# Recommender tower on one core: two more tables looked up by matmul at the start, gathered units prepared four blocks ahead, and the folded Gram values turned by DMA

## What is computed

```python
e = jnp.stack([tbl_f[ids[:, f]] for f in range(26)], axis=1)        # (2048, 26, 128)
all_emb = jnp.concatenate([r_bottom_output[:, None, :], e], axis=1)
gram = jnp.einsum('bfd,bgd->bfg', all_emb, all_emb)
z = gram[:, _TRIU_I, _TRIU_J]                                        # (2048, 351)
h = jnp.concatenate([z, r_bottom_output], axis=1)                    # (2048, 479)
h = jnp.maximum(h @ W_top1 + b_top1, 0.0)                            # 512
h = jnp.maximum(h @ W_top2 + b_top2, 0.0)                            # 256
y = h @ W_top3                                                       # 1
```

## Time and profile before

| | |
|---|---|
| median of 3 runs | 356.62 us (356.36 to 359.17) |
| the profiled execution | 355.85 us, of which the span is 354.1 us |
| busy: TensorE, VectorE, ScalarE, GpSimd | 329.4, 245.1, 205.0, 255.7 us |
| TensorE's granted clock | full throughout |
| DMA | 42.88 MB, 121 GB/s on average |

### The profile page before, as it was taken

One profiled execution on the slowest core, in us unless ns is written; L12 is line 12 of the kernel. 1 busy time (PEld: TensorE's weight loads), 2 busy tenths in 40 slices (PEclk: granted clock), 3 DMA queues, 4 the chain that ended last, 5 costly groups with the idle time before them and its releaser, 6 DMA issues.

```text
span 354.1 us, 13649 instructions
## 1 busy us (share of the span) xinstructions
PE 329.4 (93%) x5840; PEld 295.9 (84%) x5840; DVE 245.1 (69%) x720; ACT 205.0 (58%) x349; POOL 255.7 (72%) x274
## 2 busy tenths in 40 slices
PE   0788989999999999999999989999999999999996
PEld 0676979998888989979888889879999798888885
DVE  1999989996676978459763987549885597431412
ACT  3684777522345659549478567565865587572222
POOL 5777777777777777777777777777777777777720
PEclk9999999999999999999999999999999999999999
DMA  6668649422228685576685496584769476532210
GB/s 206 189 173 219 184 127 316 121 55 54 55 54 159 95 165 114 83 155 136 148 115 98 98 175 123 121 99 99 158 125 141 99 130 113 115 83 56 56 31 1
DMA packets 64203, 42.88 MB, mean 121 GB/s; under 512 B 48784, under 2 KB 56464, under 8 KB 64016
## 3 DMA queue, kind: packets, MB, share of 16 engines
q1 hardware_dynamic: 55024, 24.38, 34.8%
q0 software_dynamic: 8448, 17.32, 20.8%
q10 hardware_dynamic: 672, 0.33, 0.3%
HBM read 31.24 MB, written 0.01 MB: 88 GB/s over the span
## 4 chain that ended last, share of the span: by engine, by line
PE 82%; DVE 9%; DMA 3%; ACT 2%; issue 2%; SPq 0%; ACTq 0%; DVEq 0%
PE hot_ps L498 30%; PE gram_ps L476 14%; PE h_ps L530 11%; PE xt_ps L498 9%; PE h_ps L575 8%; DVE onehot L731 5%; PE h_ps L527 4%; PE xt_ps L459 3%; DMA rows_sb<-in_rows_dram 2%; DVE tab L798 2%; PE zt_ps L512 2%; DMA ids_wide<-in_hot_ids_dram 1%; DVE h L788 1%; ACT turned L993 1%; DVE Z L739 1%
## 5 line engine op out<-in xcount | busy, mean ns | idle before, releaser
L445 POOL DMA_INDIRECT X<-in_table_dram,rows_sb x264 | 254.3, 963 | 82.8 <-issue 78.9
L731 DVE TENSOR_SCALAR onehot<-ids_wide,row_value 128x288 fp32r<-128x288 int16 (+2 forms) x575 | 183.9, 390 | 31.6 <-PE hot_ps L498 20.6
L498 PE MATMUL hot_ps<-onehot,tab 128*128 128x288 f32 (+2 forms) x948 | 144.6, 305 | 14.1 <-DVE onehot L731 13.8
L498 PEld LDWEIGHTS hot_ps<-onehot,tab 128*128 128x128 f32 x948 | 132.0, 190 | 17.7 <-issue 15.4
L706 ACT COPY XT<-turned 128x512 int16<-128x512 int16 x82 | 65.7, 885 | 8.7 <-DMA turned<-planes 8.7
L883 ACT COPY XT<-hot_ps 128x288 f32<-128x288 f32 (+2 forms) x66 | 40.1, 658 | 39.8 <-PE hot_ps L498 37.5
L476 PEld LDWEIGHTS gram_ps<-XT 128*27 128x27 f32 x4096 | 45.1, 104 | 20.9 <-issue 15.8
L476 PE MATMUL gram_ps<-XT 128*27 128x26 f32 x4096 | 56.3, 192 | 4.2 <-issue 1.2
L872 ACT COPY planes<-X 128x1024 int16<-128x1024 int16 x41 | 44.3, 1082 | 17.5 <-DMA X<-in_table_dram,rows_sb 17.5
L530 PE MATMUL h_ps<-stage_sb,w_sb 128*128 128x256 f32 (+3 forms) x192 | 44.2, 366 | 0.0
L530 PEld LDWEIGHTS h_ps<-stage_sb,w_sb 128*128 128x128 f32 (+1 forms) x192 | 35.0, 191 | 4.3
(11 more groups left out here) (54 smaller groups left out, 137.8 us busy)
## 6 DMA issues: line engine op xcount, KB each, us to landing
stage_sb<-in_hot_dram SPq DMA_DIRECT2D x20, 256.0 KB, 3.5
X<-in_table_dram,rows_sb POOLq DMA_INDIRECT x264
ids_wide<-in_hot_ids_dram SPq DMA_DIRECT2D x8, 360.0 KB, 5.3
ids_wide<-in_hot_ids_dram SPq DMA_DIRECT2D x4, 400.0 KB, 4.0
bottomT<-in_bottom_t_dram SPq DMA_DIRECT2D x8, 128.0 KB, 3.9
w_sb<-in_w_dram SPq DMA_DIRECT2D x1, 1024.0 KB, 7.0
turned<-planes SPq DMA_TRANSPOSE x41
stage_sb<-in_hot_dram SPq DMA_DIRECT2D x5, 128.0 KB, 2.9
```

What stands on the lines that cost most here:

```text
L445: pool.indirect_dma_start(X[:, n % RING, k, :], None, table, bass.IndirectOffsetOnAxis(idx[:, column:column + 1], 0)).then_inc(gathered[n ...
L498: mm = pe.matmul(hot_bank(i)[:, 0:width(n)], tab[u][:, part, D * c:D * (c + 1)], onehot[p % ONEHOTS][:, c - BITES[u][h], 0:width(n)], star ...
L731: compared = dve.tensor_scalar(onehot[p % ONEHOTS][:, c - BITES[u][h], 0:width(n)], ids_wide[:, k, 0:width(n)], row_value[:, c:c + 1], Non ...
```

## The change

Sizes. GATHERED stays 16; EXTRA is 2, so 8 hot tables are looked up in the head (140 products) and 2 are gathered for its eight blocks, by one SIDE unit of four gathers into a view of Z, with its own indices (`side_sb`). 260 gathers in all. Order of the units: 0, 1, SIDE, 2, ... 63; turned in the head behind tables 1, 2, 4, 6 and 7. The hot tables' pieces start with two of 2 chunks for table 0; 6 instead of 12 pieces are split behind the head, in 3 steps.

Ahead. Units are split, turned and, where TensorE turns them, transposed in step b for block b+4 (LEAD) instead of b+2 and b+1. Blocks 10 to 59 go by DMA.

Folded values. For tiles 0 to 12 ScalarE splits the folded columns into 16-bit halves (`split_z`), SP starts a DMA transpose (`turn_z`, behind the unit's turn), and VectorE puts the halves together in ZT by two int16 copies. Tiles 13 to 15 go by TensorE as before.

TensorE. All blocks to 55 go in pairs (`pair`), strips always in runs of 16; both layer-1 products or both layer-2 products of a step stand on end. Layer 2 has half a bank for each tile of a pair, and VectorE works in that half instead of in SBUF. The last eight blocks are reordered. VectorE's memset of gram_ps and the addition to the long list of row numbers move behind other work in the head.

```diff
-ALWAYS = 16
-SOMETIMES = 4
-HOT = TABLES - ALWAYS
-HOT_BASE = HOT - SOMETIMES
+GATHERED = 16
+EXTRA = 2
+HOT = TABLES - GATHERED
+HOT_BASE = HOT - EXTRA
 FOUR = 4
 BLOCKS = P // PAD
-TILE_COLUMNS = BLOCKS * (1 + ALWAYS // FOUR)
-BOTTOM_SLOT = ALWAYS + SOMETIMES
+TILE_COLUMNS = BLOCKS * GATHERED // FOUR
...
-SPLIT_STEPS = 6
+SPLIT_STEPS = 3
...
+LEAD = 4
+SIDE = UNITS
+STREAM = [0, 1, SIDE] + list(range(2, UNITS))
+HEAD_TURNS = {1: 0, 2: 1, 4: SIDE, 6: 2, 7: 3}
+Z_BY_DMA = TILES - 3
+TURN_FROM, TURN_TO = 10, UNITS - BLOCKS
+BY_DMA = list(range(TURN_FROM, TURN_TO))
+DIRECT = [n for n in STREAM if n not in BY_DMA]
 NTH = {n: k for order in (DIRECT, BY_DMA) for k, n in enumerate(order)}
+MOVED = {n: k + 1 for k, n in enumerate(STREAM)}
...
+            def turn_z(t):
+
+                sp.wait_ge(z_split, t + 1)
+                wait(sp, zt_moved, t)
+                sp.dma_start_transpose(z_turned[:].rearrange("p h c s -> p (h c) s"),
+                                       z_planes[:].rearrange("p h c s -> p (h c s)")).then_inc(z_turned_in, 16)
...
+            for b in range(LAST):
                 n = GROUP_OF[b]
+                if b == STARTS[n + 1] - 3 and n + 2 < GROUPS:
+                    load_low_ids(n + 2)
+                if b == STARTS[n] and 0 < n < GROUPS - 1:
                     load_high_ids(n + 1)
+                if b + LEAD in BY_DMA:
+                    turn(b + LEAD)
+                if b % BLOCKS == 0 and 0 < b // BLOCKS <= Z_BY_DMA:
+                    turn_z(b // BLOCKS - 1)
...
+            for n in STREAM:
+                if n == BLOCKS:
                     pool.wait_ge(idx_ready, 1)
+                if n == SIDE:
+                    pool.wait_ge(side_ready, 1)
+                    for k in range(FOUR):
+                        pool.indirect_dma_start(side[:, k, :], None, table,
+                                                bass.IndirectOffsetOnAxis(side_sb[:, k:k + 1], 0)
+                                                ).then_inc(side_gathered, 16)
+                    continue
                 before = n - RING
                 if before >= 0 and before in BY_DMA:
                     pool.wait_ge(planes_ready, NTH[before] + 1)
                 elif before >= 0:
                     pool.wait_ge(xt_full, NTH[before] + 1)
                 for k in range(FOUR):
-                    column = TILE_COLUMNS * t + (k if j is None else BLOCKS + FOUR * j + k)
+                    column = FOUR * n + k
...
+                if begin == 0 and (t % 2 == 0 or t >= TILES - 2):
+                    wait(pe, prod_done, t)
...
+            def layers(t, j):
 
                 g = t // 2 - 1
+                if g < 0:
+                    return
+                if t % 2 == 0 and j == 2:
+                    layer1(g, 0)
+                    layer1(g, 1)
+                if t % 2 == 1 and j == 0:
+                    layer1(g, 2)
+                    layer1(g, 3)
+                if t % 2 == 1 and j == 2:
+                    layer2(2 * g)
+                    layer2(2 * g + 1)
+
+            def pair(b):
+
                 t, j = b // BLOCKS, b % BLOCKS
+                between = t >= 2 and (t % 2 == 1 or j == 2) and b + 2 < LAST
+                if between:
                     lookups(*slice_of(b))
+                    strips(b, 0, 1)
+                    layers(t, j)
+                    strips(b, 1, RUNS)
                 else:
                     for run in range(RUNS):
                         lookups(*slice_of(b, run, run + 1))
+                        strips(b, run, run + 1)
+                if b + LEAD < TURN_FROM:
+                    transposes(b + LEAD)
+                for run in range(RUNS):
+                    lookups(*slice_of(b + 1, run, run + 1))
+                    strips(b + 1, run, run + 1)
+                if not between:
+                    layers(t, j)
+                if j == 0 and t > 0:
+                    z_transposes(t - 1)
+                if b + 1 + LEAD < TURN_FROM:
+                    transposes(b + 1 + LEAD)
...
             def last_blocks():
+                b, t = LAST, TILES - 2
                 pe.wait_ge(hot_placed, 1 + max(i for i in range(len(LOOKUPS)) if hot_bank(i) is xt_ps))
+                strips(b)
+                strips(b + 1, 0, 1)
                 z_transposes(t - 1)
+                strips(b + 1, 1, RUNS)
                 layer1(len(JOBS) - 3, 0)
                 layer1(len(JOBS) - 3, 1)
+                strips(b + 2, 0, 1)
+                transposes(b + 4)
+                strips(b + 2, 1, RUNS)
                 layer1(len(JOBS) - 3, 2)
                 layer1(len(JOBS) - 3, 3)
+                strips(b + 3, 0, 1)
+                transposes(b + 5)
+                strips(b + 3, 1, RUNS)
                 layer2(t - 2)
+                z_transposes(t)
+                layer2(t - 1)
                 b, t = LAST + BLOCKS, TILES - 1
+                strips(b, 0, 1)
+                transposes(b + 2)
+                strips(b, 1, RUNS)
                 layer1(len(JOBS) - 2, 0)
                 layer1(len(JOBS) - 2, 1)
+                strips(b + 1)
                 layer1(len(JOBS) - 2, 2)
                 layer1(len(JOBS) - 2, 3)
+                transposes(b + 3)
+                strips(b + 2)
+                strips(b + 3)
                 bottoms_last(0, C1 - 1)
+                layer2(t - 1)
                 z_transpose_last(0)
                 z_transpose_last(1)
                 bottoms_last(C1 - 1, C1)
...
             def move_zt(t):
 
                 g, at = JOB_OF[t]
-                dve.wait_ge(zt_full, t + 1)
+                if t >= Z_BY_DMA:
+                    dve.wait_ge(zt_full, t + 1 - Z_BY_DMA)
+                else:
+                    dve.wait_ge(z_turned_in, 16 * (t + 1))
                 if t == 0:
                     dve.wait_ge(part1, FIRST_PIECE[HOT])
                 wait(dve, h1_full, C1 * (g - 1))
+                if t < Z_BY_DMA:
+                    for h in range(2):
+                        moved = dve.tensor_copy(ZT_words[g % 2][:, :, at, :, h], z_turned[:, h, :, :])
+                    moved.then_inc(zt_moved, 1)
+                    return
...
-                dve.wait_ge(h2_full, t + 1)
+                dve.wait_ge(h2_full, t + 1 if t >= TILES - 2 else t + 2 - t % 2)
                 wait(dve, prod_done, t)
-                dve.tensor_tensor(h2[:], h2_ps[:, 0:N2], vec_sb[:, 0, :], ALU.add).then_inc(h2_moved, 1)
+                h2 = h2_half(t)
+                dve.tensor_tensor(h2, h2, vec_sb[:, 0, :], ALU.add).then_inc(h2_moved, 1)
                 dve.wait_ge(h2_moved, t + 1)
-                dve.scalar_tensor_tensor(h2[:], h2[:], 0.0, vec_sb[:, 1, :], ALU.max, ALU.mult,
+                dve.scalar_tensor_tensor(h2, h2, 0.0, vec_sb[:, 1, :], ALU.max, ALU.mult,
...
             for q in range(FIRST_PIECE[HOT_BASE]):
-                split_second(q)
+                if q == FIRST_PIECE[1]:
+                    dve.wait_ge(side_loaded, 16)
+                    dve.tensor_tensor(side_sb[:, 0:FOUR], side_sb[:, 0:FOUR], side_sb[:, FOUR:2 * FOUR], ALU.add
+                                      ).then_inc(side_ready, 1)
+                    dve.wait_ge(rows_loaded, 16)
+                    dve.tensor_tensor(chunks[:, 1:, :], chunks[:, 1:, :],
+                                      starts.to_broadcast([P, TILES - 1, TILE_COLUMNS]), ALU.add).then_inc(idx_ready, 1)
                 for p in asked_of(q):
                     one_hot(p)
+                split_second(q)
+            dve.memset(gram_ps[:], 0.0).then_inc(pads_zero, 1)
...
+            def split_z(t):
+
+                if t == 0:
+                    act.wait_ge(z_pads_zero, 1)
+                act.wait_ge(folded_all, t + 1)
+                wait(act, z_turned_in, 16 * t)
+                pairs = folded[:].rearrange("p r c -> p (r c)")[:, HALF:HALF + PAIRS]
+                act.copy(z_planes[:].rearrange("p h c s -> p h (c s)")[:, :, 0:PAIRS],
+                         pairs.bitcast(i16).rearrange("p (e h) -> p h e", h=2)).then_inc(z_split, 1)
...
+                for i in placed_in(b):
+                    if i not in ended(b):
+                        place_hot(i)
                 for p in pieces_ended(b):
+                    if is_last(p) and ASKED[p][0] in placed_in(b):
+                        place_hot(ASKED[p][0])
                     one_hot_share(p + ONEHOTS)
+                if j == 0 and 0 < t <= Z_BY_DMA:
+                    split_z(t - 1)
+                split_words(b + LEAD)
                 if j == 2:
                     place_bottom(t + 1)
                 for q in LATE_PIECES[PER_STEP * b:PER_STEP * (b + 1)]:
                     split_first(q)
+                if b + LEAD < TURN_FROM:
+                    move(b + LEAD)
+                if b + LEAD - 1 in BY_DMA:
+                    move(b + LEAD - 1)
...
+                place_bottom(TILES - 1)
                 relu(len(JOBS) - 3, 0)
                 relu(len(JOBS) - 3, 1)
```

(11 more changed lines are left out.)

339 lines of the change are left out of this document (130 added, 209 removed).

## The result

The changed kernel took 370.88 us, the kernel before on the same chip 357.89: a ratio of 1.0378, 95% interval 1.0343 to 1.0412. It is slower by 3.8%. I had forecast 352.8 us and a range from 350.9 to 356.8. The profiled execution has a span of 369.8 us against 354.1, 15.7 us more. The profiled execution before took 355.85 us, less than its median, and the one of the changed kernel 371.86, more than its median; so the medians differ by 13.0 us only.

A forecast was written before the change was run, and what follows sets the result against it. Two chains, GpSimd's gathers and TensorE's own work, were taken to arrive together, the gathers deciding after the change. Last turn 337.2 + 12.8 + 0.3 gave a 350.3 us span against 354.1, in proportion 352.8 us; range 350.9 to 356.8.

The forecast's parts named there:

- Turns: TensorE, block 0 to the last turn: 9 of 22 unit turns remain, at 0.40 us each, -5.2 us.
- Transposes of folded: TensorE, block 0 to the last turn: 13 transposes of 0.31 us a tile go, -4.0 us.
- The 0.52 us waits at layer 2: TensorE: layer 2's second tile no longer waits for h2_moved, with half a bank for each tile, -2.1 us.
- The tail: Behind the last turn: 12.8 us remain as before, plus 0.3 us for the last tile's transposes.
- The gather stream: GpSimd: four gathers fewer -5.0, waits for TensorE -1.0, slower gathers +1.5; sum -4.5 us, last gather over at 334.9 us.
- part 4: End of the kernel: last unit's landing and the path from block 60's unit, 15.4 us, put the last turn at 337.2 us.
- The head: TensorE up to block 0: two more tables looked up, sum +7.8 us, block 0 at 39.3 instead of 31.5 us.
- The chain in order takes over: Rival in SP's queue: z_turned waits behind turn(b+4), delaying VectorE's one-hots; 2 to 4 us of gain lost; chance 0.12.
- TensorE's 5 us as spare: End of the kernel: TensorE's 5 us of spare time goes into waits for gathered rows.
- the term of the runs in part 3: TensorE, block 0 to the last turn: runs of 16 strips save 0.24 us a pair, -4.7 us, ends 0 and -9.
- The order of the bounds: Whole kernel: gathers and TensorE's work arrive together before; after the change the gathers decide, TensorE waiting for gathered rows.

The follow-up runs named there:

- e3: The changed kernel with layer 1 and layer 2 two blocks later, relus and layer 3 moved with them; 360.56 us, ratio 1.0080 to the kernel before.
- e1: The changed kernel with the folded values of all tiles turned on TensorE again; 358.44 us, ratio 1.0035 to the kernel before.
- e2: The changed kernel with SP issuing the transpose of the folded values ahead of the turn of unit b+4; 357.66 us, ratio 0.9998.
- b1: The kernel before with only half_tile changed: lookups and strips of both blocks in runs of 16 strips; 371.4 us, ratio 1.0407.
- e4c: The kernel of e2 with strips in runs of 32 instead of 16, a repeat run; 355.61 us, ratio 0.9955 to the kernel before.
- e6b: The later layers of e3 with e2's order in SP's queue and units 4 to 9 turned three blocks ahead; 360.51 us, ratio 1.0086.
- e5b: The kernel of e2 with units 4 to 9 turned three blocks ahead instead of four; 357.56 us, ratio 1.0006 to the kernel before.

## Why the prediction was wrong

**What held.** Turns: -5.5 us measured, -5.2 counted. Transposes of folded: -4.4, -4.0 counted. The 0.52 us waits at layer 2 went, 2.1 us. The tail is 13.2 us, 13.1 counted. The gather stream: its last start at 333.2 to 336.6 us in the kernels of the change in which ScalarE held it for no more than 0.3 us at a time, 334.0 counted (its end at 334.9 less 0.94). The path of part 4 from the turn of block 60's unit to the last turn: 16.2 us, 15.4 counted. The head was dearer in the sum than in fact: block 0 came 5.0 us later and not 7.8, since VectorE made its first split at 5.59 us instead of 9.05 and I had counted 1 us for that.

**The step that failed** is the price and the place of the rival "The chain in order takes over", and with it the sentence of part 4 that counts TensorE's 5 us as spare. The mechanism was there, in the right queue: turn_z behind turn(b+4). But I had it arrive at VectorE's one-hots, with "about 1 us a tile" for every second tile, and gave it 2 to 4 us and a chance of 0.12. It arrives at layer 1, which I never set against it: layer 1 of a pair of tiles stands in the second pair of blocks of the next tile, 7.8 to 9.2 us behind the fold, while from the fold's end to the end of the copy it takes 9.4 to 12.0 us. In the first case, 12.0: 1.4 until ScalarE begins the split, 0.7 for it, 1.0 for the unit's split, 1.4 for the turn's issue ahead in the queue, 6.4 from the issue to the copy, and 1.05 for the copy. Each of six pairs of tiles missed by 0.5 to 3.7 us, 12.4 in all, and the lower clock, behind two of these waits and one for gathered rows, added 5.1. (The one-hots, where I had looked for it, are waited for only in e3, with layer 1 out of the way: 2.9 us.) e1, which takes the chain out, is 12.4 us faster, and e2, which shortens it, 13.2. I had checked durations on each engine and the spare time in sum, but not when the result of the new path is due.

**The second step** is the term of the runs in part 3, -4.7 us. In e2, where nothing else disturbs it much, lookups, strips and layer 1 together are 264.4 us against 262.4 before: +2.0. The strips did fall, by 9.2 us with the block that was moved; but the lookups, in 48 more runs, cost 8.3 more, and layer 1 between two strip runs 2.9 more. In b1, where layer 1 stands behind short runs and not between them, it costs 0.4 more. e4c, with runs of 32, has 259.9. Three readings made the term: the row with two widths taken for one (b1 above), an average of 1.93 us for 64 strips that has 0.07 us of idle time in it, and no price for layer 1 in its new place. That is 6.7 us of the forecast's relief of TensorE. It fits with e1 and e2 ending level with the kernel before, not 4 us below, with the last turn 7 us behind the last gather's end: TensorE, not the gathers, bounds them.

Together this is the whole distance. By itself TensorE was to begin the last turn at 331.6 us and began it at 356.6, 25.0 us later: 12.4 of waits at layer 1, 5.1 of half clock, 6.7 of runs and layer 1's place, and 4.0 of other idle time that I had taken as gone, less 2.8 of head and some tenths.

**The order of the bounds** was thus wrong from the start for the change as made: GpSimd set its pace in the first blocks at most (2.1 us of TensorE's waits are for gathered rows) and later waited 5.5 us for ScalarE. With both faults mended (e4c) the gathers and ScalarE behind them hold the kernel up to 310 us of 352 and TensorE's own work from there, at 355.6 us.

What stays open: why the later layers of e3 and e6b, with layer 1 freed of its wait, bring one long wait of TensorE elsewhere; that wait and the clock behind it are what they lose against e2 and e5b.

## What to carry to other kernels

When work is moved from a busy engine to a DMA, add up the whole path to its first reader (split, queue, whatever stands ahead in the queue, transfer, copy) and hold it against the moment at which that reader is due; the spare time of the engine in sum doesn't cover a date that is missed each time. In an in-order queue the short transfer that somebody waits for goes ahead of the one that is needed four blocks later. Shorter runs of one kind of matmul mean more starts for the runs between them; count both sides, for every width that occurs, and look at each instruction before a row that groups forty of them is used as a price.

## What was not expected of the hardware

- In the changed kernel waits of TensorE of 1.72, 3.68 and 3.22 us were each followed by 3.4 us at half clock (2.99 us for 1.70, 2.77 for 1.46), while waits of 2.07 and 1.96 us there, and of 1.92 and 2.37 us in e2, were not.
- A DMA transpose of 128 x 768 int16 took 3.5 to 7.5 us from its issue to the copy of its result, over the tiles of the changed kernel for which VectorE stood waiting, and going first in the queue didn't shorten it (e2); the profile of the kernel before couldn't have told me, since it lists no time to landing for transposes.
- Small fp32 matmuls of 27 columns (two records each) cost 11.0 ns a record in runs of 32 records, 12.9 in runs of 64 (e4c) and 14.6 in the runs of 128 of the kernel before.
